# SBUF buffers begin at multiples of 128 bytes instead of 32, in a cross-attention block on one core

## The reference

```python
xn = _adaln(x, noise_emb, ln1_w, ln1_b)            # (x-mu)*rsqrt(var+eps)*(1+gamma)+beta, gamma/beta from cond
q, k, v = jnp.split(xn @ qkv_w.T, 3, axis=-1)      # then rope on q and k, 16 heads
x = x + _attn(q, k, v) @ sa_out_w.T
xn = _adaln(x, noise_emb, ln2_w, ln2_b)
q = _rope((xn @ q_w.T)...); k = _rope((context @ k_w.T)...); v = context @ v_w.T
x = x + _attn(q, k, v) @ ca_out_w.T
xn = _adaln(x, noise_emb, ln3_w, ln3_b)
h = jax.nn.gelu(xn @ ffn_w1.T + ffn_b1, approximate=False)
x = x + (h @ ffn_w2.T + ffn_b2)
```

## Time and profile before

| | |
|---|---|
| median of three runs | 1907.29 us |
| the profiled execution's own time | 1905.51 us |
| its span, from the first to the last instruction | 1903.4 us |
| PE busy | 1867.2 us, 98% of the span |
| ACT busy | 1429.7 us, 75% |
| DVE busy | 1285.6 us, 68% |
| POOL busy | 801.9 us, 42% |
| TensorE clock granted | 0.998 of full speed |
| main DMA queue | 306576 packets, 308.67 MB, 56.0% of 16 engines' span |

### The profile page before, as it was taken

One profiled execution on the slowest core, in us unless ns is written; L12 is line 12 of the kernel. 1 busy time (PEld: TensorE's weight loads), 2 busy tenths in 40 slices (PEclk: granted clock), 3 DMA queues, 4 the chain that ended last, 5 costly groups with the idle time before them and its releaser, 6 DMA issues. The chain is left out here.

```text
span 1903.4 us, 38411 instructions
## 1 busy us (share of the span) xinstructions
PE 1867.2 (98%) x13460; PEld 1631.8 (86%) x13460; DVE 1285.6 (68%) x2241; ACT 1429.7 (75%) x3811; POOL 801.9 (42%) x834
## 2 busy tenths in 40 slices
PE   8899999999999999999999999999999999999999
PEld 7788888888878888988988987688898988989898
DVE  5877666767777776776776776346766667666754
ACT  5788878888888898888888899655656566666654
POOL 3534333433443454454454444104535445353531
PEclk9999999999999999999999999999999999999999
DMA  7777777676687687677677688433131322323131
GB/s 219 206 210 209 216 207 204 188 206 188 186 232 212 196 236 221 192 222 220 190 217 223 193 226 201 130 111 122 56 111 56 112 78 93 97 73 105 46 99 34
DMA packets 307375, 311.46 MB, mean 164 GB/s; under 512 B 22000, under 2 KB 259952, under 8 KB 307184
## 3 DMA queue, kind: packets, MB, share of 16 engines
q1 hardware_dynamic: 306576, 308.67, 56.0%
q10 hardware_dynamic: 608, 0.34, 0.1%
HBM read 212.46 MB, written 92.27 MB: 160 GB/s over the span
## 5 line engine op out<-in xcount | busy, mean ns | idle before, releaser
L769 ACT ACTIVATE ps_s<-ps_s,neg_max 128x256 f32<-128x256 f32 x1024 | 461.6, 454 | 52.0 <-DVE neg_max L884 48.8
L884 DVE TENSOR_REDUCE neg_max<-ps_s 128x2 f32<-128x512 f32 x512 | 349.1, 686 | 202.7 <-PE ps_s L640 202.0
L783 ACT ACTIVATE prob<-ps_s 128x512 f32<-128x512 f32 x512 | 307.8, 602 | 89.2 <-PE ps_s L661 85.0
L965 POOL TENSOR_TENSOR rope_c<-rope_c,rope_s 128x256 f32<-128x256 f32 x128 | 98.5, 769 | 316.1 <-DVE rope_s L859 316.1
L640 PE MATMUL ps_s<-kT,qT 96*128 96x256 f32 x1024 | 218.1, 294 | 9.2 <-ACT ps_s L769 4.9
L769 ACT ACTIVATION_READ_ACCUMULATOR ps_s<-ps_s,neg_max 128x1 f32 x1024 | 217.7, 213 | 0.0
L640 PEld LDWEIGHTS ps_s<-kT,qT 96*128 96x128 f32 x1024 | 168.4, 190 | 56.9 <-ACT ps_s L769 21.9
L661 PE MATMUL ps_s<-qT,kT 112*128 112x256 f32 x1024 | 207.7, 285 | 9.6 <-ACT ps_s L769 8.8
L630 PE MATMUL ps_g<-xx_hi,w_hi 128*128 128x256 f32 x1024 | 208.7, 285 | 1.8 <-issue 1.4
L630 PE MATMUL ps_g<-xx_hi,w_lo 128*128 128x256 f32 x1024 | 206.1, 283 | 0.0
L630 PE MATMUL ps_g<-xx_lo,w_hi 128*128 128x256 f32 x1024 | 205.7, 282 | 0.0
(11 more groups left out here) (157 smaller groups left out, 4714.3 us busy)
## 6 DMA issues: line engine op xcount, KB each, us to landing
kT<-k_turned SPq DMA_DIRECT2D x384, 128.0 KB, 3.3
qT<-q_turned SPq DMA_DIRECT2D x128, 256.0 KB, 4.0
f_raw<-in_w1T SPq DMA_DIRECT2D x124, 256.0 KB, 3.0
k_turned<-rot_hi SPq DMA_DIRECT2D x64, 256.0 KB, 3.2
k_turned<-rot_lo SPq DMA_DIRECT2D x64, 256.0 KB, 2.5
q_turned<-rot_hi SPq DMA_DIRECT2D x64, 256.0 KB, 3.8
q_turned<-rot_lo SPq DMA_DIRECT2D x64, 256.0 KB, 4.2
qT<-q_turned SPq DMA_DIRECT2D x128, 128.0 KB, 4.1
```

What stands on the lines that cost most here:

```text
L769: ins = eng.activation(scores[:, t * L:(t + 1) * L], scores[:, t * L:(t + 1) * L], ACT.Exp, bias=neg_max[G % 2][:, t, j:j + 1], accum_out= ...
L783: eng.activation(prob[:, n % NP, :, :].rearrange("p t l -> p (t l)"), ps_s[:, score_bank(step), :], ACT.Exp).then_inc(exp_done, 1)
L884: eng.tensor_reduce(neg_max[G % 2][:, :, j], ps_s[:, score_bank(step), :].rearrange("p (t l) -> p t l", l=L), AX.X, ALU.max, negate=True). ...
L965: eng.tensor_tensor(rope_c[n % 2][:, 0, :], rope_c[n % 2][:, 0, :], rope_s[:, 0, :], ALU.subtract)
```

## The change

All three helpers ask for `align_bytes=128`. Nothing else is changed. The programs of before and after have the same instructions in the same order on each engine, with the same operands, shapes, waits and semaphores, and only the places of the buffers differ.

```diff
@@ -28,6 +28,8 @@
+LINE = 128
@@ -347,7 +349,7 @@
         def keep(name, shape, dt=F32):
-            return whole.enter_context(nc.sbuf_tensor(name, shape, dt))
+            return whole.enter_context(nc.sbuf_tensor(name, shape, dt, align_bytes=LINE))
@@ -378,7 +380,7 @@
             def sb(name, shape, dt=F32):
-                return stage.enter_context(nc.sbuf_tensor(name, shape, dt))
+                return stage.enter_context(nc.sbuf_tensor(name, shape, dt, align_bytes=LINE))
```

## The result

The changed kernel took 1910.97 us, the median of 13 runs (1908.57 to 1913.55), against 1906.06 us of the kernel before (13 runs, 1904.18 to 1907.54). The ratio is 1.0025, with a 95% interval of [1.0017, 1.0034]. That is 4.9 us more. The time lies within the forecast range. The loss is clear of zero, and at 0.25% it lies just beyond the 0.2% that the forecast called no change, though the interval reaches down to 0.17%: by its middle value it is the slower case, which the prediction gave a chance of 0.06.

A forecast was written before the change was run, and what follows sets the result against it. TensorE's instruction times were taken to bound the kernel. Terms of 0 for every engine and the DMAs left the median of 1907.3 us unchanged, with a range of 1903.0 to 1912.0 us.

The forecast's parts named there:

- the slower case: Whole kernel: slower by more than about 0.2% (3.8 us), the slow rival with other losses of that size; chance 0.06.
- What bounds the kernel: Whole execution: TensorE's products cover 1867.2 of 1903.4 us, so its instructions set the time; shorter waits give at most 36.2 us.
- TensorE at 0: TensorE's products: operands beginning at multiples of 128 cost 0; bound 0.4% of 1867.2 us, 7 us to either side.
- The slow rival: Line 1320: operands with equal rests cost 2 ns on each of 2352 products, 4.7 us, giving 1912.0 us; chance 0.06.
- The chance of 0.06: Chance given to the slow rival on line 1320 (4.7 us), with other losses of that size.
- VectorE, ScalarE, GpSimd and DMA at 0: Work beside TensorE: alignment changes none of these; bounds 1% on VectorE and ScalarE, 0.5 us on a DMA.
- The weight loads of the values: Line 676: 2048 loads stop straddling a multiple of 128, taken as 0; if uncovered, 1 ns each, 2 us.
- The fast rivals: TensorE reads rest 0 faster, up to 7 us, chance 0.05; POOL speeds up, up to 5 us, 0.02 in the time.
- The profile's mark for the slow one: Line 1320's product time in the changed profile: a rise from 283 to 285 ns would show the slow rival holds.

The follow-up runs named there:

- e4: The changed kernel, with all large buffers at multiples of 128, but w_hi and w_lo 64 bytes further; 1911.58 us, ratio 1.0030 to the kernel before.
- e2: The changed kernel, with all large buffers at multiples of 128, but the cw buffers 64 bytes further; 1901.13 us, ratio 0.9972 to the kernel before.
- e7: Kernel before with chosen distances: xx 64 off w, kT off qT, cw off xf and xx; h, w equal modulo 512; 1897.87 us, ratio 0.9949.
- e8: Kernel before with cw alone moved, so xf - cw is 32 modulo 512 instead of 192; 1904.60 us, ratio 0.9990.
- e10: Kernel before with h_hi and h_lo alone moved, so w and h are 64 apart modulo 512 instead of 256; 1900.56 us, ratio 0.9976.
- e9: As e7, but kT and qT a multiple of 128 apart and cw 32 from xf and xx; 1901.60 us, ratio 0.9979 to the kernel before.
- e12: As e7, but w and h 64 apart modulo 512 instead of 0; 1901.72 us, ratio 0.9979 to the kernel before.
- e6: Kernel before with cw alone moved, so xf - cw is 128 modulo 512 instead of 192; 1913.72 us, ratio 1.0037.
- e5: Kernel before with one 96-byte gap ahead of w_hi, shifting all that follows and keeping its distances; 1907.24 us, ratio 1.0003.

## Why the prediction was right or wrong

- **What bounds the kernel** held. PE's own instructions set the time, the waits hardly moved, and the whole result is in how long the products take.
- **TensorE at 0** is the step that failed. It compared rests of one operand (`xn` at 0 against `v_kept` at 96, with `ident` at 0 in both), found 272 and 272 ns, and these rows did stay. The pairs differed in their distances too, 0 modulo 128 in one and 96 from `ident` to `v_kept` in the other, so the transposes care for neither; the mistake was to carry a comparison of transposes with 128 columns over to products with 256. The measured term is a distance, and for line 1320 it is +0.09 us on 4.24 us, 2% where I had bounded all of TensorE by 0.4%.
- **The slow rival** was the right mechanism with the right line. It put the price at 2 ns for 2352 products, 4.7 us, and 1912.0 us. Measured: 4.33 - 4.24 = 0.09 us on each burst of 36 and 0.02 us on each of 6, 2.6 ns a product, 56 x 0.11 = 6 us, and 0.02 us on each of the two groups of 12 of line 1336, another 2 us that it did not have. PE's 8.8 us more in feed-forward, less 1.2 us of waits that vanish, less 1.0 us in attention, are the 6.6 us of the profiled executions. It came out near its number by luck as well, because two terms that it left out, line 1336 and attention, have opposite signs. The measured 1910.97 us also looks nearer to the forecast of 1907.3 us than the change was, because that forecast came from three runs whose median lay 1.2 us above the 13-run median of the kernel before.
- **The chance of 0.06** was too low. I set the difference of 285 and 283 ns between lines 630 and 1320 aside, because the first runs among waits. The median of line 630, 283 ns against line 1320's 281 ns in the same trace, does not suffer from the waits and would have answered that. e4 shows it as well: with xx and w 64 apart two of line 630's three kinds drop to 279 ns. Equal rests are not the whole condition, though: line 1336 had them before (32 and 32) with 2.75 us for its 12 products, and in e4, with 64 and 0, it took 2.80 us.
- **VectorE, ScalarE, GpSimd and DMA at 0** were right: 540/957 ns, 1293 ns and landings as before. The 950 ns of `v_kept` had nothing to do with its rest.
- **The weight loads of the values** kept 106/110 ns on `v_kept` whether they straddle a multiple of 128 or not.
- **The fast rivals** did not come with this change, although 4 to 9 us were there for other layouts (e2, e7, e10). The profile's mark for the slow one ("should 1320 rise to 285, the slow rival holds") was met at 283 to 284 ns.

## What to carry to other kernels

Where TensorE is busy all the time, look at where the two operands of its products begin relative to each other, and not at how each is aligned. An alignment common to all buffers takes away differences that may be worth keeping; here it cost 0.25%, and 64 bytes put back between two groups of buffers (e2) gave 0.3% over the kernel before. A layout is to be tried whole, though: the gains of e8 and e10 did not add to those of e7 (e9, e12).

To see such a thing, read the pace of a stretch in which PE never waits (36 products in 4.24 or 4.33 us in the chain), or add up the times from start to start by line, since means and busy sums of overlapping products show it only dimly.

## What the runs showed of the hardware that I had not expected

- A 256-column product on 128x128 weights, in float32 as the profile has it, starts 113.6 to 120.3 ns after the last one, on average over an unbroken burst, with nothing altered but where buffers lie (4.09 us in e10, 4.33 us in the changed kernel and e6, for 36 products).
- The pattern repeats: e5, with the starts moved by 96 bytes, has 4.24 us for each burst of 36 and 10.44 us from one burst to the next, as the kernel before has. That the two also fall on the same 1809.52 us is chance, since attention ended 1.1 us earlier in e5 and feed-forward was 1.0 us longer.
- The pace of a line can depend on a buffer that it does not read (e10: h moved, line 1320 from 117.8 to 113.6 ns), and on what ran before it (e12: 12 products of line 1336 in 2.79 us behind 36 products of line 1320 and in 2.76 us behind 6).
